# Low parts beside the experts: from VectorE to GpSimd, in an attention and mixture-of-experts kernel

## The reference

```
x  = layernorm(x)                       # 4 x 1024 tokens, 256 channels
attention: 16 heads of 4 sequences; two softmax maps per head (8 channels each);
           o = a1 - lambda * a2; rms norm; projection; bias
experts:   logits = tokens @ wg; the two best of 8 experts per token, capacity C = 1024 rows
           disp[e]  = the rows sent to expert e                  (1024 x 256)
           h[e]     = gelu(disp[e] @ w_gate[e])                  (1024 x 1024)
           eo[e]    = h[e] @ w_down[e]                           (1024 x 256)
           out      = g1 * eo[f1] + g2 * eo[f2]
return x + attention + experts
```

## Time and profile before

| | us |
|---|---|
| median of 3 runs | 1752.04 |
| lowest and highest run | 1750.6 and 1752.13 |
| span of the profiled execution | 1749.3 |
| TensorE busy in it | 1697.2 (97%) |
| VectorE busy | 1503.2 (86%) |
| ScalarE busy | 1397.3 (80%) |
| GpSimd busy | 537.6 (31%) |

### The profile page before, as it was taken

One profiled execution on the slowest core, in us unless ns is written; L12 is line 12 of the kernel. 1 busy time (PEld: TensorE's weight loads), 2 busy tenths in 40 slices (PEclk: granted clock), 3 DMA queues, 4 the chain that ended last, 5 costly groups with the idle time before them and its releaser, 6 DMA issues.

```text
span 1749.3 us, 38531 instructions
## 1 busy us (share of the span) xinstructions
PE 1697.2 (97%) x15106; PEld 722.6 (41%) x15107; DVE 1503.2 (86%) x1792; ACT 1397.3 (80%) x2637; POOL 537.6 (31%) x1098
## 2 busy tenths in 40 slices
PE   6999999999999999999999999999999999999999
PEld 5557777777773222222222222222222222222227
DVE  7878787787777999999999999999999999999935
ACT  4464534544546999999999999999999999999994
POOL 1124111111000243332433323425534233443344
PEclk9989999999999999999999999999999999999999
DMA  8754333321203111111111111111111111100003
GB/s 261 219 193 137 106 105 103 107 75 54 85 25 115 34 31 41 30 37 36 29 40 32 34 32 35 38 34 33 39 30 36 36 31 39 32 22 14 11 11 103
DMA packets 92276, 109.60 MB, mean 63 GB/s; under 512 B 17472, under 2 KB 67264, under 8 KB 92096
## 3 DMA queue, kind: packets, MB, share of 16 engines
q1 hardware_dynamic: 85952, 90.36, 16.6%
q0 software_dynamic: 6144, 16.79, 3.3%
HBM read 72.77 MB, written 33.82 MB: 61 GB/s over the span
## 4 chain that ended last, share of the span: by engine, by line
PE 67%; ACT 28%; DVE 3%; issue 1%; DMA 1%; ACTq 0%; SPq 0%; DVEq 0%
ACT arena_t L853 25%; PE banks L1326 19%; PE banks L1314 12%; PE banks L1363 10%; PE banks L1296 8%; PE banks L1341 7%; PE banks L1343 4%; PE banks L1406 2%; ACT o_raw L836 2%; PE banks L1199 2%; PE banks L1442 1%; PE banks L1242 1%; DVE rest L951 1%; PE banks L1231 1%; DVE arena_q L958 1%
## 5 line engine op out<-in xcount | busy, mean ns | idle before, releaser
L1066 DVE TENSOR_REDUCE row_half<-banks 128x2 f32<-128x1024 f32 x1024 | 1186.5, 1216 | 81.9 <-PE banks L1296 80.0
L853 ACT ACTIVATE arena_t<-banks 128x512 f32<-128x512 f32 x2048 | 1083.2, 599 | 42.0 <-PE banks L1314 16.5
L1326 PE MATMUL banks<-arena_t,v_ring 128*17 128x256 f32 x8192 | 642.3, 386 | 25.6 <-ACT o_raw L836 25.5
L1326 PEld LDWEIGHTS banks<-arena_t,v_ring 128*17 128x17 f32 x8192 | 136.1, 95 | 408.0 <-issue 240.3
L1314 PE MATMUL banks<-arena_q 50*128 50x512 bf16 x960 | 284.1, 383 | 0.0
L1296 PE MATMUL banks<-arena_q 48*128 48x512 bf16 x960 | 268.5, 384 | 0.2 <-DVE row_half L1066 0.2
L1314 PE MATMUL banks<-qk_ring 50*128 50x512 bf16 x896 | 264.1, 385 | 1.6 <-DVE arena_r L1094 1.5
L1296 PE MATMUL banks<-qk_ring 48*128 48x512 bf16 x896 | 248.6, 382 | 0.0
L818 ACT ACTIVATE arena_t<-banks 128x512 f32<-128x512 f32 x128 | 76.6, 598 | 199.1 <-PE banks L1363 188.0
L1341 PE MATMUL banks<-w_parts,hidden_parts 128*128 128x512 f32 x512 | 186.9, 406 | 1.6 <-DVE arena_r L1094 1.6
L1363 PE MATMUL banks<-rows_parts,w_parts 128*128 128x512 f32 x768 | 183.2, 394 | 2.5 <-DVE rows_parts L1010 2.5
(11 more groups left out here) (150 smaller groups left out, 1488.1 us busy)
## 6 DMA issues: line engine op xcount, KB each, us to landing
expert_rows<-arena_r SPq DMA_DIRECT2D x16, 512.0 KB, 3.2
q_stack<-arena_q SPq DMA_DIRECT2D x8, 768.0 KB, 3.5
k_stack<-arena_q SPq DMA_DIRECT2D x8, 768.0 KB, 4.4
v_ring<-v_heads SPq DMA_DIRECT2D x64, 68.0 KB, 2.9
arena_x<-x_in SPq DMA_DIRECT2D x4, 1024.0 KB, 6.3
token_rows<-arena_x SPq DMA_DIRECT2D x4, 1024.0 KB, 4.8
arena_v<-w_gate_in SPq DMA_DIRECT2D x4, 1024.0 KB, 6.3
arena_v<-w_down_in SPq DMA_DIRECT2D x4, 1024.0 KB, 8.7
```

What stands on the lines that cost most here:

```text
L853: nc.scalar.activation(probs[:, kt % PSLOTS, q, :], banks[:, ST_BANKS[ring_place(i) % 3], :], ACT.Exp).then_inc(exp_done, 1)
L1066: nc.vector.tensor_reduce(halves[:, :, j // 2], banks[:, smax_bank(m):smax_bank(m) + 2, :], AX.X, ALU.max, negate=True).then_inc(smax_done, 1)
L1326: mm = pe.matmul(banks[QUAD * q:QUAD * q + VP, OT_BANK, columns], v_ring[:, g % SLOTS, kt, :], probs[:, kt % PSLOTS, q, columns], start=(k ...
```

## The change

Six of the eight low parts of a chunk's Gelu rows (f = 0 to 5) and the low part of the next expert's weights are issued by GpSimd instead of VectorE. In GpSimd's loop they stand ahead of `find_rows` and `neg_split`. The low parts of f = 6 and 7 stay with VectorE and count on a semaphore of their own, for which TensorE waits. The functions have the same operands as before.

```diff
+POOL_LOWS = 6
...
+        last_hidden_ready = sem("last_hidden_ready")
...
+            def hidden_low(n, f):
+
+                pool.wait_ge(hidden_high, FC * n + f + 1)
+                nc.gpsimd.tensor_tensor(hidden_parts[:, LO, f, :], hidden[:, LO, f, :], hidden_parts[:, HI, f, :].bitcast(F32),
+                                        ALU.subtract).then_inc(hidden_ready, 1)
+
+            def next_weights_low(n):
+
+                s, which = 1 - n // 2 % 2, n % 2
+                pool.wait_ge(w_high, n + 1)
+                nc.gpsimd.tensor_tensor(w_parts[s][:, which, LO], w_ring[s][:, which, LO], w_parts[s][:, which, HI].bitcast(F32),
+                                        ALU.subtract).then_inc(w_low, 1)
+
             for n in range(2 * E):
+                for f in range(POOL_LOWS):
+                    hidden_low(n, f)
+                if n // 2 + 1 < E:
+                    next_weights_low(n)
                 if n + 2 < 2 * E:
                     find_rows(n + 2)
                 if n % 2 == 0 and n > 0:
                     neg_split(n // 2 - 1)
...
             def expert_step(n):
                 e, s = n // 2, n % 2
                 for f in range(FC):
-                    dve.wait_ge(hidden_high, FC * n + f + 1)
-
-                    nc.vector.tensor_tensor(hidden_parts[:, LO, f, :], hidden[:, LO, f, :], hidden_parts[:, HI, f, :].bitcast(F32),
-                                            ALU.subtract).then_inc(hidden_ready, 1)
+                    if f >= POOL_LOWS:
+                        dve.wait_ge(hidden_high, FC * n + f + 1)
+                        nc.vector.tensor_tensor(hidden_parts[:, LO, f, :], hidden[:, LO, f, :], hidden_parts[:, HI, f, :].bitcast(F32),
+                                                ALU.subtract).then_inc(last_hidden_ready, 1)
...
                 for m in range(3, 6):
                     smax(8 * n + m)
-                if e + 1 < E:
-                    next_weights_low(n)
                 smax(8 * n + 6)
...
-                if t == 0:
-                    pe.wait_ge(hidden_ready, FC * n + f + 1)
+                if t == 0 and f < POOL_LOWS:
+                    pe.wait_ge(hidden_ready, POOL_LOWS * n + f + 1)
+                elif t == 0:
+                    pe.wait_ge(last_hidden_ready, (FC - POOL_LOWS) * n + f - POOL_LOWS + 1)
```

More of the change, by code:

```diff
@@ L1081, in neg_turn @@
                 nc.vector.transpose(neg_blocks[:, g % 2, :], neg_parts[:, g % 2].rearrange("p s a t -> p (s a t)")).then_inc(neg_turned, 1)
[L1083 to L1088, removed]
             def down_sum(n, t):
```

## The result

The changed kernel takes 1821.81 us (median of 4 runs, 1820.91 to 1822.64), against 1752.01 before: a ratio of 1.0404, interval 1.0389 to 1.0419. The profiled execution's span grew from 1749.3 to 1820.1 us, by 70.8. The prediction was 1824 us, and 71.6 for the span.

A forecast was written before the change was run, and what follows sets the result against it. TensorE's own stream was taken to bound the experts. Six even chunks (+66.6 us), chunk 0 (+6.6) and lost small waits (-1.6) gave +71.6, a span of 1820.9 and a time of 1824 us; range 1807 to 1842.

The forecast's parts named there:

- The bound: Expert chunks: TensorE's own stream bounds them; taking work off VectorE can win only 1.6 us.
- The queue ahead of `neg_split`: Even chunks 2 to 12: `neg_split` comes after weights' part and gathers, delaying `neg_turn` and low 6; TensorE idles 9.3 us.
- Per chunk: Six even chunks with weights: 9.7 us of delay plus 1.4 us for the clock each, 66.6 us in all.
- the clock's price: TensorE after each 9.3 us stall: falling to half speed costs 1.9 us, of which 1.4 are added.
- Chunk 0: GpSimd's six lows start only after its memsets, at 140.3; TensorE ends its down pairs 6.6 us later.
- five waits of 0.6 us: Expected sign in chunk 0: after waiting some 4 us, TensorE waits five times 0.6 us for GpSimd's lows.
- The clock holds: Rival: TensorE's clock stays up in the six 9.3 us stalls; 8.4 us less, 1815 us; chance 0.17.
- The two engines hold each other up over SBUF: Rival: GpSimd's weights' part delays VectorE's `rows_t_low` in seven odd chunks; 18 us more, 1842 us; chance 0.08.
- Not slower: Rival: GpSimd's queue ends before TensorE reaches f = 6, so both stalls are absent; 1750.4 us; chance 0.03.

The follow-up runs named there:

- mended: split_first with chunk 0's six GpSimd hidden low parts issued ahead of the memsets of the last head slots; 1748.98 us, ratio 0.9994 to the kernel before.
- split_first: Changed kernel with GpSimd's `neg_split` first in its chunk instead of last; 1756.13 us, ratio 1.0031 to the kernel before.
- turn_late: Changed kernel with VectorE's `neg_turn` last in an even chunk instead of at f = 4, GpSimd's queue untouched; 1755.14 us, one profiled run.
- gathers_first: Changed kernel with the four gathers first in GpSimd's chunk and `neg_split` still last; 1797.5 us (two runs).
- weights_vector: Changed kernel with the next weights' low part given back to VectorE, the six hidden low parts staying on GpSimd; 1765.73 us (two runs).
- filled: Changed kernel with 36 spare TensorE matmuls ahead of f = 6 of the down tiles in even chunks 2 to 12; 1812.13 us, ratio 1.0344 to the kernel before.
- filled_chunk0: split_first with 15 spare TensorE matmuls ahead of chunk 0's first down pair; 1755.13 us, ratio 1.0020 to the kernel before.

## Why the prediction was right

*The bound.* TensorE's stream bounds the experts: VectorE's 86 us less bought 1.7 us once the new waits were gone (mended). Right.

*The queue ahead of `neg_split`.* Right in its place and in its parts: split_first takes it away at GpSimd, turn_late at VectorE, and each returns 66 us (66.4 and 66.5 over chunks 1 to 14 of the traces); gathers_first and weights_vector shorten it by 4.9 and 7.8 us and TensorE's waits with it, one for one. GpSimd's weights' part took 4.57 us on the mean for the estimated 4.59, the gathers' pitch was 1.25, a hidden low 1.29 for 1.27. The wait was 8.9 us where 9.3 were worked out: the first gather came 0.15 us after the subtraction and not 0.30, the turn and low 6 overlap by 0.1 us, and the view counts from the end of the last pair.

*Per chunk.* 9.7 us was forecast for the wait with what follows it, and 9.45 found (filled). For the clock 1.4 was forecast, and 1.6 found on the mean. The sum over six chunks was 66.6, the finding 66.3. That it is so close is in part luck: the wait was sized 0.25 us too long and the clock 0.2 too short, and the clock's price, one number in the prediction, went from 1.0 to 2.4 us.

*Chunk 0.* 6.6 forecast, 6.7 found. But the prediction's picture in it, five waits of 0.6 us, was wrong for the changed kernel: TensorE never waited again after 3.75 us, as its clock had fallen and its pairs took as long as GpSimd's lows. At full clock the records show waits of 0.27 to 0.28 us (filled_chunk0), half of what lies between GpSimd's pitch of 1.24 and the 0.71 us of two pairs; the matmul after a wait is drawn longer there (0.50 us for 0.40). The prediction had a fall of the clock here as an addition, up to 9 us for the chunk; the fall came and cost nothing, as GpSimd's pace hid it. The size didn't depend on it.

*The rivals.* "The clock holds" fell: the clock row shows 0.50. "The two engines hold each other up over SBUF" fell as a cost: in odd chunks `rows_t_low` took 1.29 us and began as early as before (15.7 us into its chunk, as at 348.51 in the earlier trace rows), beside GpSimd's 4.6 us; it has one input in SBUF. The timeline of chunk 3, which starts at 221.50 (VectorE, then GpSimd):

```profile
237.24 1.29 DVE L1029 TENSOR_TENSOR rows_parts<-banks,rows_parts 128x512 fp32r<-128x512 f32 x2 [1.60 <-ACT rows_parts L787]
...
236.80 4.59 POOL L715 TENSOR_TENSOR w_parts<-arena_v,w_parts 128x2048 fp32r<-128x2048 f32 x1 [3.23 <-ACT w_parts L832]
```

"Not slower" fell as the changed kernel stands. Its 1.6 us of gain is what the mended order shows (1748.98 us beside a kernel before of 1750.49), though that difference is not clear of the noise.

What stays open: 0.7 us at the start of chunk 0 and -1.3 us in attention are differences between single profiles; no run looked into them.

## What to carry to other kernels

When work moves to an idle engine, don't ask only whether it has the time; write down its new order, and for each instruction already there who waits for it. A long instruction ahead of a short one that another engine's queue waits for costs its full length as soon as nothing covers the delay any more, and so does every wait that it brings along (here 3.2 us for ScalarE). Of the 17 us that VectorE stood here, 8.9 reached TensorE; the rest was covered. Put the short, awaited instruction first. And a stall on TensorE costs more than its length: here 9.45 us of it cost 11 on the mean, because the clock fell.

## What the runs showed of the hardware

That one of the two engines can hold up the other, which the prediction had only in one direction, shows in the other too. In chunk 1 of the changed kernel, small VectorE operations with two inputs in SBUF ran into GpSimd's hidden lows. The timelines of GpSimd and of VectorE there:

```profile
160.90 4.03 POOL L708 TENSOR_TENSOR hidden_parts<-arena_t,hidden_parts 128x512 fp32r<-128x512 f32 x3 [3.14 <-ACT hidden_parts L839]
...
161.11 1.14 DVE L1072 TENSOR_TENSOR lam_diff<-lam_exp 128x1 f32<-128x1 f32 x1
162.30 0.15 DVE L1074 TENSOR_SCALAR half_factor<-lam_diff 128x1 f32<-128x1 f32 x1
...
162.48 1.15 DVE L1075 TENSOR_TENSOR gates<-gates,keep 128x64 f32<-128x64 f32 x1
```

L1072 works on one column and took 0.16 us before, L1075 took 0.23; each ended within 0.1 us of the end of the hidden low beside it (162.24 and 163.56). The operation between them, with one input tensor, took its usual 0.15. This is what the Trainium skill says ("SBUF — State Buffer", Who interferes with whom): a VectorE instruction with two inputs in SBUF waits for a GpSimd instruction that reads there, to its end. The trace agrees. Here it cost nothing: chunk 1 takes 25.82 us.

TensorE's clock fell in each of the six idle stretches of 8.9 us and in or just behind each of the six of 4.0 us (gathers_first), and in none of the six of 1.1 us (weights_vector). The price was not the same each time: 1.0 to 2.4 us behind equal stalls in one run. It goes with how long the clock stays low once TensorE works again. Two windows of the changed kernel, each eight microseconds of full work right behind a stall, of chunk 2 and of chunk 12:

```profile
209.91:217.91 8.00, 8.00 (x30) 5.57 (x30) 6.52 (x8) 0.00 (x0) 0.00 (x0) 0.61 0.00 1
523.76:531.76 8.00, 8.00 (x38) 5.63 (x39) 7.43 (x9) 0.00 (x0) 0.00 (x0) 0.81 0.00 0
```

A mean of 0.61 is 6.2 us at 0.50, and one of 0.81 is 3.0 us. In the same way chunks 2, 4, ..., 12 have 6.2, 4.1, 3.0, 5.8, 3.9 and 3.0 us at the low level, and cost 2.4, 1.5, 1.0, 2.3, 1.4 and 1.0 us beyond filled's 35.27.

The length of the idle stretch is not all that counts. In the kernel before, TensorE stood for 1.50 us between the experts and attention (from 538.39), and the clock was at 0.50 from 543 us on, three microseconds after it had resumed, in other work than the experts':

```profile
543.00:546.00 3.00, 2.98 (x19) 0.48 (x23) 2.22 (x2) 1.82 (x4) 0.00 (x0) 0.50 1.07 365
```
